# A second layer's bias moved from the scatter into the second layer: openers over row tiles, and a buffer laid into another

## What is computed

```python
B, S, D, G = 2, 4096, 512, 32; NEXPERTS, SETS, ESIZE = 32, 4, 32      # here taken as 16 batches of 1024 tokens
x = layernorm(x)
logits = einsum('bntd,des->bntes', grouped, Wc) + bc + tie            # groups of 32 tokens, 128 expert sets
perm = (logits == max(logits, axis=-3))                               # in each group, each set picks one token
permuted = einsum('bntd,bntes->bnesd', grouped, perm)
inner = relu(einsum('bnesd,esdf->bnesf', permuted, W1) + b1)
result_permuted = einsum('bnesf,esdf->bnesd', inner, W2) + b2         # b2: one row of 512 for each of 128 sets
result = einsum('bnesd,bntes->bntd', result_permuted, perm)
out = x + tanh(g_ffn) * result
```

## Time and profile before

| | before |
|---|---|
| median of 3 runs | 2039.99 us (2036.7 to 2043.06) |
| profiled execution | 2038.99 us, span 2037.2 us, mean granted clock 0.973 |
| PE / PEld busy | 1826.3 us (90%) / 1282.2 us (63%) |
| DVE / ACT / POOL busy | 1413.5 us (69%) / 876.4 us (43%) / 260.2 us (13%) |
| L1058 + L1059 (b2 in the scatter), PE | 63.8 + 51.6 us, 128 of each |
| L1062 (rest of the scatter), PE | 139.1 us, 1024 records |
| L1045 (second layer), PE | 96.0 + 57.2 us, 4096 records |

### The profile page before, as it was taken

The page is one execution under the profiler, slowest core; times in us unless marked ns, Lnnn a source line. Parts: engine busy times, 40 slices in busy tenths (PEclk is TensorE's granted clock), DMA queues, the critical chain, the costliest instruction groups (busy, mean ns, idle before and its releaser), DMA issues.

```text
span 2037.2 us, 53514 instructions
## 1 busy us (share of the span) xinstructions
PE 1826.3 (90%) x23504; PEld 1282.2 (63%) x23504; DVE 1413.5 (69%) x2114; ACT 876.4 (43%) x1126; POOL 260.2 (13%) x624
## 2 busy tenths in 40 slices
PE   6699999999999999868889988998888898889885
PEld 3377777777777777656665566566656665665551
DVE  4177777777777777634776668667756766686666
ACT  2533333333333333235445544544554454545531
POOL 0122222222222222101100110111011001100100
PEclk9799999999999999979999999999999999999997
DMA  7412323333332323135645765575457547655752
GB/s 233 171 52 95 115 95 118 113 122 116 119 116 95 115 95 128 50 132 226 248 158 198 270 224 170 211 270 217 156 210 265 188 169 253 240 178 187 270 183 88
DMA packets 123814, 339.24 MB, mean 167 GB/s; under 512 B 10304, under 2 KB 18240, under 8 KB 106176
## 3 DMA queue, kind: packets, MB, share of 16 engines
q1 hardware_dynamic: 123584, 335.82, 46.2%
HBM read 259.23 MB, written 76.55 MB: 165 GB/s over the span
## 4 chain that ended last, share of the span: by engine, by line
PE 37%; DVE 7%; DMA 5%; issue 4%; ACT 3%; SPq 0%; POOL 0%; DVEq 0%
PE ps L1024 13%; PE ps L998 7%; PE ps L969 4%; PE ps L1062 4%; DMA out<-y 4%; PE ps L1045 4%; DVE res L924 3%; PE ps L963 3%; DMA y<-x_scratch 1%; PE ps L1058 1%; DVE gat L885 1%; PE ps L1059 1%; DVE res L879 1%; ACT gat L825 1%; ACT gat L820 1%
## 5 line engine op out<-in xcount | busy, mean ns | idle before, releaser
L879 DVE STREAM_TRANSPOSE res<-res 128x2048 f32<-128x2048 f32 x128 | 292.1, 2295 | 0.1
L820 ACT ACTIVATE gat<-ps 128x1536 f32<-128x1536 f32 (+1 forms) x128 | 172.2, 1345 | 222.8 <-PE ps L998 222.8
L892 DVE SCALAR_TENSOR_TENSOR y<-ps,gate_f,y 128x512 f32<-128x512 f32 x128 | 95.2, 744 | 209.5 <-DMA y<-x_scratch 152.4
L559 PE MATMUL ps<-xTh,qh 128*128 128x512 f32 x512 | 203.0, 397 | 1.4 <-DVE xTl L486 1.4
L1024 PE MATMUL ps<-gat,ring 128*64 128x64 f32 x5120 | 176.7, 227 | 27.4 <-issue 27.3
L559 PE MATMUL ps<-xTh,ql 128*128 128x512 f32 x512 | 200.6, 392 | 0.0
L559 PE MATMUL ps<-xTl,qh 128*128 128x512 f32 x512 | 200.4, 391 | 0.0
L1024 PEld LDWEIGHTS ps<-gat,ring 128*64 128x64 f32 x5120 | 163.7, 141 | 38.0 <-issue 30.6
L998 PE MATMUL ps<-sel,xn 32*128 32x128 f32 x4096 | 154.9, 286 | 31.7 <-ACT sel L842 18.6
L998 PEld LDWEIGHTS ps<-sel,xn 32*128 32x128 f32 x4096 | 131.1, 188 | 67.3 <-ACT gat L820 43.1
L924 DVE COPY res<-ps 128x1024 f32<-128x1024 f32 x128 | 151.7, 1220 | 20.1 <-PE ps L1045 19.7
(11 more groups left out here) (117 smaller groups left out, 3268.2 us busy)
## 6 DMA issues: line engine op xcount, KB each, us to landing
ring<-in_W SPq DMA_DIRECT2D x80, 1024.0 KB, 5.7
gat<-in_W SPq DMA_DIRECT2D x48, 1024.0 KB, 9.3
xin<-in_x SPq DMA_DIRECT2D x32, 1024.0 KB, 5.8
x_scratch<-xin SPq DMA_DIRECT2D x32, 1024.0 KB, 4.3
xn<-x_scratch SPq DMA_DIRECT2D x64, 512.0 KB, 6.4
y<-x_scratch SPq DMA_DIRECT2D x128, 256.0 KB, 3.9
out<-y SPq DMA_DIRECT2D x128, 256.0 KB, 3.9
vw_scratch<-cx SPq DMA_DIRECT2D x16, 512.0 KB, 2.6
```

The lines of the kernel that those rows point to most:

```text
L559: last = e.matmul(ps[:, 2 + n % 2, :], a[:, c, n * DH:(n + 1) * DH], b[:, c, :], start=(k == 0), stop=(k == len(parts) - 1))
L820: e.activation(o, v, ACT.Copy).then_inc(m_gaA.sem, 1)
L879: e.transpose(v, v).then_inc(m_tr.sem, 1)
L892: e.scalar_tensor_tensor(out=v, in0=ps[:, 4 + t % 4, :], scalar=gate_f[:], in1=v, op0=ALU.mult, op1=ALU.add).then_inc(m_fin.sem, 1)
```

## The change

b2 leaves the scatter. Before the first round it is loaded in another layout (b2s, 128 x 2 x 512): each set's row stands twice in every block of 32 partitions, and after three DVE instructions one copy holds the rounded part and the other the remainder. `rowk` holds for each u a 32-row selector of zeros and ones. `outer` now begins with four openers: f32r matmuls of 32 rows and 128 columns, one to each of its four banks, that lay both parts of b2 into all 128 partitions; the 16 tiles then add to them. `scatter` keeps its four f32 matmuls. The buffer `lgt` is no tensor of its own any more, but the second half of `sel`. Two of the table `beside`'s places move.

```diff
-        b2h = sb0("b2h", [P, D], F32R)
-        b2l = sb0("b2l", [P, D], F32R)
+        b2s = sb0("b2s", [P, 2, D], F32R)
+        rowk = sb0("rowk", [P, 4, P], F32R)
+        part = sb0("part", [P, 18])
...
-        lgt = sb("lgt", [P, HT])
+        lgt = sel[:, TH:, :].rearrange("p t e -> p (t e)")
...
-        beside = [[], [], [("T", 0)], [("T", 1), ("lg", 0)], [("T", 2), ("lg", 1), ("T", 3), ("lg", 2)],
-                  [("T", 4), ("lg", 3), ("T", 5), ("lg", 4)], [("T", 6), ("lg", 5)],
-                  [("T", 7), ("lg", 6), ("lg", 7), ("sT", 0)]]
+        beside = [[], [], [], [("T", 0)], [("T", 1), ("lg", 0), ("T", 2), ("lg", 1)], [("T", 3), ("lg", 2), ("T", 4), ("lg", 3)],
+                  [("T", 5), ("lg", 4), ("T", 6), ("lg", 5)], [("T", 7), ("lg", 6), ("lg", 7), ("sT", 0)]]
...
-            e.dma_start(y[:, 0], b2_dram).then_inc(d_b2.sem, 16)
+            e.dma_start(y[:, 0:2], b2_dram).then_inc(d_b2.sem, 16)
...
-            e.activation(b2h[:], y[:, 0], ACT.Copy).then_inc(m_b2h.sem, 1)
+            e.activation(rowk[:].rearrange("p u (k n) -> p (u k) n", k=4), part[:, 0:16].unsqueeze(2).broadcast_to([P, 16, NG]), ACT.Copy)
+            e.activation(b2s[:], y[:, 0:2], ACT.Copy).then_inc(m_b2h.sem, 1)
...
-            e.tensor_tensor(b2l[:], y[:, 0], b2h[:].bitcast(F32), ALU.subtract).then_inc(m_b2l.sem, 1)
+            e.tensor_tensor(y[:, 2:4], y[:, 0:2], b2s[:].bitcast(F32), ALU.subtract).then_inc(m_b2l.sem, 1)
+            e.wait_ge(m_b2l.sem, m_b2l.at(0, 0))
+            e.tensor_scalar(y[:, 2:4], y[:, 2:4], part[:, 17:18], None, ALU.mult).then_inc(m_b2l.sem, 1)
+            e.wait_ge(m_b2l.sem, m_b2l.at(0, 1))
+            e.scalar_tensor_tensor(out=b2s[:], in0=b2s[:].bitcast(F32), scalar=part[:, 16:17], in1=y[:, 2:4],
+                                   op0=ALU.mult, op1=ALU.add).then_inc(m_b2s.sem, 1)
...
             def outer(i, u):
...
+                e.wait_ge(m_b2s.sem, m_b2s.at(0))
+                for j in range(4):
+                    r = slice(j * F, (j + 1) * F)
+                    e.matmul(ps[:, bank(u) + j, :], rowk[r, u // 2, :], b2s[r, u % 2, :],
+                             start=True, stop=False, skip_group_check=True)
                 for k in range(4):
                     for j in range(4):
                         r = slice(j * F, (j + 1) * F)
-                        last = e.matmul(ps[k * NG:(k + 1) * NG, bank(u) + j, :], hid[r, 8 * k + u, :], second(u)[r, k, :], start=True, stop=True)
+                        last = e.matmul(ps[k * NG:(k + 1) * NG, bank(u) + j, :], hid[r, 8 * k + u, :], second(u)[r, k, :],
+                                        start=False, stop=True, skip_group_check=True)
...
-                e.matmul(ps[:, 4 + t % 4, :], s, b2h[:], start=True, stop=False, skip_group_check=True)
-                e.matmul(ps[:, 4 + t % 4, :], s, b2l[:], start=False, stop=False, skip_group_check=True)
...
-                                    start=False, stop=(g == GT - 1), skip_group_check=True)
+                                    start=True, stop=True, skip_group_check=True)
```

More of the change, by code:

```diff
@@ L52, in build @@
 def build(nc, x, ctx_in, mask, gx_in, gf_in, rms, q_w, kv_w, out_w, Wc, bc, W1, b1, W2, b2,
-          ident_in, cos_in, sin_in, tie_in, out):
+          ident_in, cos_in, sin_in, tie_in, part_in, out):
     x1_dram = nc.dram_tensor("x1_scratch", (B, T, D), F32, kind="Internal").ap()
@@ L74, in build @@
         b1r = sb0("b1r", [P, P])
-        b2h = sb0("b2h", [P, D], F32R)
-        b2l = sb0("b2l", [P, D], F32R)
+        b2s = sb0("b2s", [P, 2, D], F32R)
+        rowk = sb0("rowk", [P, 4, P], F32R)
+        part = sb0("part", [P, 18])
         tie = sb0("tie", [P, G])
-        consts = (wc, bcol, b1r, b2h, b2l, tie)
+        consts = (wc, bcol, b1r, b2s, rowk, part, tie)
         const_loads = [(wc, Wc.rearrange("(c p) e s -> p c (e s)", p=P)), (bcol, bc),
-                       (tie, tie_in.partition_broadcast(P))]
+                       (tie, tie_in.partition_broadcast(P)), (part, part_in)]
         const_loads += [(b1r[s * Q:(s + 1) * Q], b1) for s in range(4)]
@@ L93, in build @@
             attention(nc, top, ps, ident, small, cos, sin, qh, ql, xin, kept, kept_loads, x, kr_dram, vw_dram, x1_dram)
-        experts(nc, top, ps, kept, consts, ident, small, gate_f, x1_dram, W1, W2, b2.rearrange("e s d -> (e s) d"), out)
+        experts(nc, top, ps, kept, consts, ident, small, gate_f, x1_dram, W1, W2, b2, out)
 def unit_tokens(d, u):
@@ L171, in _ @@
                 e.dma_start(vw_dram[b], vwb[:, b % VB]).then_inc(d_vws[b % VB].sem, 16)
-            e.wait_ge(d_const.sem, d_const.at(0, 6))
+            e.wait_ge(d_const.sem, d_const.at(0, 7))
             e.wait_ge(d_x.sem, d_x.at(0, RING - 1))
@@ L658, in experts @@
         NY = 4
-        wc, bcol, b1r, b2h, b2l, tie = consts
+        wc, bcol, b1r, b2s, rowk, part, tie = consts
         xn = sb("xn", [P, NT, D])
@@ L678, in experts @@
         d_yl, d_ys = ([mark(f"{n}{k}", 1, 16) for k in range(NY)] for n in ("yl", "ys"))
-        d_b2, m_b2h, m_b2l = mark("b2", 1, 16), mark("b2h"), mark("b2l")
+        d_b2, m_b2h, m_b2l, m_b2s = mark("b2", 1, 16), mark("b2h"), mark("b2l", 2), mark("b2s")
         d_ring = [mark(f"ring{k}", 1, 16) for k in range(2)]
@@ L1050, in scatter @@
                     e.wait_ge(m_tr.sem, m_tr.at(i, 7))
-                    e.wait_ge(m_b2l.sem, m_b2l.at(0))
                 if t >= 4:
@@ L1103 @@
     b1 = np.asarray(L0_ffn_b1).reshape(Q, P)
+    b2 = np.asarray(L0_ffn_b2).reshape(4, 4, 2, 4, D).transpose(3, 1, 0, 2, 4)
+    b2 = np.stack([b2, b2], axis=2).reshape(P, 2, D)
+    row = np.arange(F)
+    part = np.zeros((4, F, 18), np.float32)
+    part[:, row, row // 8 * 4 + row % 4] = 1.0
+    part[:, row, 16 + row // 4 % 2] = 1.0
+    part = part.reshape(P, 18)
     arrays = {
@@ L1107 @@
         "rms": np.asarray(L0_xattn_rms_scale).reshape(C, P).T, "q_w": L0_xattn_q_w, "kv_w": L0_xattn_kv_w, "out_w": L0_xattn_out_w,
-        "Wc": L0_ffn_Wc, "bc": np.asarray(L0_ffn_bc).reshape(E, 1), "W1": w1, "b1": b1, "W2": w2, "b2": L0_ffn_b2,
-        "ident": np.eye(P, dtype=np.float32), "cos": cos, "sin": sin, "tie": tie,
+        "Wc": L0_ffn_Wc, "bc": np.asarray(L0_ffn_bc).reshape(E, 1), "W1": w1, "b1": b1, "W2": w2, "b2": b2,
+        "ident": np.eye(P, dtype=np.float32), "cos": cos, "sin": sin, "tie": tie, "part": part,
     }
```

10 lines of the change are left out of this document (5 added, 5 removed).

## The result

| | before | change |
|---|---|---|
| median | 2039.74 us (2036.70 to 2043.06, 4 runs) | 2060.64 us (2053.08 to 2065.91, 4 runs) |
| profiled execution | 2038.99 us, span 2037.2 us | 2056.33 us, span 2054.5 us |
| mean granted clock | 0.973 | 0.962 |

The account below looks back on a forecast made before the run. The prediction saw PE and y's DMA/DVE chain ending the scatter stage close together, with the DMA backlog, not PE, dating later `finish` steps. It summed 2039.0 - 12 + 27 + 4.5 - 2 = 2056.5, forecast 2056 us, range 2036 to 2084.

Parts of the forecast that it names:

- b2 out of the scatter: Scatter stage: PE loses 82 us of work, of which only an earlier second `pick` and eighth `finish` count, -12 us.
- I take half, 3 us: Eighth `finish`: waits for PE in three rounds, worth up to 6 us over all rounds; half of that is counted.
- every landing follows by one b2 share: Scatter stage, upper bound: y's stores leave earlier by 0.64 us and all landings follow, another 9 us, -24 us in all.
- against: Scatter stage: 9.5 us from y's store to next load at full DMA engines; 9.0 us in all before the second `pick`.
- Openers: Second layer: 0.48 us per opener up to the first tile, 1.69 us per round, +27 us over 16 rounds.
- The first pair: First two outers of the second layer: free, as DVE needs 3.47 us and PE 3.39, a cover of 0.08 us.
- b2's making: Before the first round: extra load, ACT and DVE work on b2 delay the statistics by 4.5 us, between 3 and 6.
- The end: Last batch's scatters: 3.6 us less b2 work, some 1.5 us given back at half clock, -2 us (-3.6 to 0).
- Rival 1: Second layer: the array empties at each change of tile shape, opener 0.75 us, +60 us, 2089 us; chance 0.13.
- rival 4: Second layer: row tiles don't overlap in f32r, opener 4 x 0.31 us, at least +100 us, 2130 or more; chance 0.04.
- Rival 2: Second layer: openers stay near one matmul's time, 0.31 us, +15 us, 2044.5 us, no change; chance 0.22.
- Rival 3: Scatter stage: y's loads follow the scatters, `outer(0)` up to 4.1 us earlier in 14 rounds, 2011 us; chance 0.10.

Follow-up runs that it names:

- a0_change: The changed kernel run again unaltered, beside other experiments on one chip: 2057.48 us, ratio 1.0071 to the kernel before.
- a1_change_again: The changed kernel run once more unaltered, on the chip of e9_filled: 2057.88 us, ratio 1.0103 to the kernel before.
- e9_filled: The changed kernel with four f32r matmuls nobody reads before outer(0) in rounds 1 to 14: 2043.2 us, ratio 1.0023 to the kernel before.
- e2_y_first: The changed kernel with 2 MB of weight loads in SP's queue moved from ahead of y's first store to behind y's eighth load: 2005.07 us, ratio 0.9816.
- e1_no_b2: The changed kernel without its openers, so b2 is left out of the result: 2021.24 us, ratio 0.9891 to the kernel before.
- e7_old_order: e2_y_first with three scatters ahead of the first turn instead of four, as before the change: 2028.0 us, ratio 0.9937 to the kernel before.
- e5_twice: e2_y_first with every outer's four openers issued twice in a row, adding b2 twice: 2026.31 us, ratio 0.9935 to the kernel before.

## Why the prediction was right, and where it was not

2056 us with 2036 to 2084 was forecast; the profiled execution took 2056.3, the median is 2060.6, and it is slower by over 0.3%. The sum fits the profiled execution to 0.2 us, but two of its terms are off by some 7 and 10 us, and a third thing was left out. That they cancel is luck.

- **b2 out of the scatter, -12 us: measured -19.0.** The place was right: y's chain stands in front. Half of it is the `pick`'s wait: from the eighth `finish` to `outer(0)` are 1.01 us in the mean instead of 1.68, 9.5 us over 14 rounds for the forecast 9.0. The step that failed is the next one, "I take half, 3 us": the eighth `finish` comes 22.59 us after the first scatter instead of 23.27, another 9.5 us. That is the size of the bound for "every landing follows by one b2 share", 9 us, but the landings do not follow like this. In the means of 14 rounds the first store leaves 0.85 us earlier after the first scatter (2.01 instead of 2.86), and the load behind it comes 0.70 us later after the store (10.96 instead of 10.26), so tile 5 is loaded 0.15 us earlier and tile 8 0.17 us (18.43 instead of 18.60). The backlog takes the lead back, as the prediction's "against" has it. The load of tile 8 then takes 4.07 us to land instead of 4.46; why stays open, and part of the 9.5 us may be scatter between executions: the eighth `finish` comes at 22.50 us in `a0_change` and at 22.92 in `a1_change_again`.
- **Openers, +27 us in 16 rounds: measured +17.2 in rounds 1 to 14 and 1.1 in round 0** (round 15's are in the last term). An opener costs 0.44 us up to its first tile (0.48 forecast), but 0.37 us in a row of outers: the next opener starts 1.07 us after the first tile (1454.53 to 1455.60), where outers before followed 1.14 us apart. So the step of two outers is not PE's, forecast as 3.24 us (2 x 1.51 = 3.02 measured), but the copies', 3.08 where it was 2.69. The step that failed is charging PE with the full distance from opener to tile twice per step. 1.23 us per round stand for the forecast 1.69. The first pair, taken as free with a cover of 0.08 us, is 0.11 us longer in the round shown.
- **Left out: the clock, +10.7 us.** The text had PE idle before `outer(0)` for the eighth `finish` and counted it as free. Idle time of PE is not free when it costs the clock of what follows, a term that the prediction put at nothing. Without it the change would have lost 6.6 us and not 17.3, and by the medians `e9_filled` takes 14.7 of 22.0 us back without touching either the openers or the scatter.
- **b2's making, +4.5 us: measured +4.2, and 1.9 that are not its own.** The start of the experts in the changed kernel:

```profile
884.83 0.35 SPq L769 DMA_DIRECT2D y<-in_b  x1
888.44 0.63 ACT L850 ACTIVATE rowk<-part 128x512 fp32r<-128x512 f32 x1 [18.51 <-DMA y<-in_b]
890.05 1.23 DVE L928 TENSOR_TENSOR y<-y,b2s 128x1024 f32<-128x1024 f32 x1 [13.26 <-ACT b2s L851]
...
893.30 1.28 DVE L898 BATCH_NORM_STATS2 b_bst<-xn 128x6 f32<-128x512 f32 x2
```

  From b2's load to the statistics are 8.47 us instead of 4.28. The load itself leaves 1.95 us later, and that is not the change: over all profiled executions of this study the first load of the experts leaves between 882.8 and 885.9 us, with no order by kernel.
- **The end, -2 us: measured 0, by three parts.** From the last batch's first scatter to the end are 18.2 us instead of 20.2, as forecast. From round 15's first gather to its `outer(0)` are 1.3 us less. But from there to that scatter are 34.2 us instead of 30.9: the last second layer has its openers, and it stands behind 12.04 us of idle PE (6.34 before) and has its first two outers wholly at the lower clock, 2.67 us each. That takes the 3.3 us back.
- **Rival 1** (0.75 us, the array empties) and **rival 4** (row tiles one after another): 0.44 us, and 0.23 us for four more; both refuted by these runs. **Rival 2** (0.31 us) was nearer to the time of an outer in a row, 0.37 us, but its 2044.5 us left out the clock. **Rival 3**: the fifth `finish` starts 15.9 us after the first scatter in the mean, far over its 13 (16.2 before); the backlog holds it, until the queue is reordered (10.7 in `e2_y_first`).

Signs that were named and came: 165 us of waits for y's loads, no wait of the `pick` for logits, PE idle before `outer(0)`. One did not: steps of 3.2 us with no gap on PE; they are 3.08 with 0.06 to spare on PE.

## What to carry over

When two paths end a stage close together, work taken off one may not be lost but banked: here it showed up as idle time, and an edit to the other path that was worth 4 us alone was then worth 52, 15 of them in clock. So try the pair before judging either. And look at what the granted clock does behind each new idle stretch of PE: here the clock cost 10.7 to 17.3 us in three executions of the change, where the extra instructions cost 17.2, and it was avoided by shortening the other path and, but for one round, even by filling the gap.

## What was not expected of the hardware

- In the three profiled executions of the change PE's granted clock fell to 0.50 (1.2 GHz) around the second layer in 27 of the 31 rounds whose idle stretch before `outer(0)` was 1.65 to 2.56 us, and in none of the 11 with 1.42 us or less. It stayed at 1.00 behind stretches as long (2.05 and 2.37 us in rounds 11 and 14 of the change), in `e1_no_b2` behind 5 of 8, and in `e7_old_order` behind 4 of 11 of 2.36 us. The Trainium skill (TensorE: Matmul & The Clock Gate, What's actually happening) names these two levels and lets idle time lower the clock. The traces agree on both; that gaps of 1.65 us and up can do it, often only when PE is at work again, is what these runs add. That the number of rounds hit varies between executions may be why the change's runs spread over 10 to 18 us in three sets and those of `e2_y_first` over 3; this is argued, not shown, and `e9_filled`, with 13 us, speaks against it being the whole cause.
- The order in one DMA queue mattered under a backlog: from the first store's issue to the load behind it were 10.96 us in the mean with 2 weight loads of 1 MB issued ahead of them, and 5.55 with these behind.
- Four f32r matmuls on row tiles of 32 rows and 128 columns, each into a bank of its own, cost 0.23 us together when they followed four others (`e5_twice`), less than the distance of 0.31 us from one on the whole array to the next.
